# A six-stage decoder in one launch: denominators first in the cross-attention, keys waited for by group, POOL's turn 1 and F1's second pair reordered

## The reference, cut to what matters

```python
x = x + _L0_attn_ref(_layernorm(x), ...)     # A0: 16 heads, softmax(q k^T) v
x = x + _L0_xattn_ref(_layernorm(x), ...)    # X0: 16 heads of 8, 77 context rows, rotary positions
x = x + _L0_ffn_ref(_layernorm(x), ...)      # F0: router to 16 experts, top 2, capacity; 2 shared experts
x = x + _L1_attn_ref(_layernorm(x), ...)     # A1: 16 heads of 8, plus clipped relative positions
x = x + _L1_xattn_ref(_layernorm(x), ...)    # X1: one head over the context
x = x + _L1_ffn_ref(_layernorm(x), ...)      # F1: 8 dense experts weighted by a top-2 gate
```

```python
attn = jax.nn.softmax(scores, axis=-1)
out = jnp.einsum('bhqk,bhkd->bhqd', attn, v)
```

```python
attn = jnp.einsum('bhld,bhrd->bhlr', q, k) * scale
rel = jnp.einsum('bhld,lrd->bhlr', q, pos_emb) * scale
attn = jax.nn.softmax(attn + rel, axis=-1)
```

## Time and profile before

| | |
|---|---|
| runs | 1357.92, 1363.59, 1365.1 us (median 1363.59) |
| profiled execution | 1360.92 us, span 1358.6 us |
| mean granted PE clock | 0.962 |
| busy: PE, DVE, ACT, POOL | 1240.3, 984.2, 711.7, 650.1 us |
| chain that ended last | PE 65%, DVE 17%, ACT 6%, issue 4%, POOL 4% |
| instructions | 29396 |

### The profile page before, as it was taken

The page is one execution under the profiler, slowest core; times in us unless marked ns, Lnnn a source line. Parts: engine busy times, 40 slices in busy tenths (PEclk is TensorE's granted clock), DMA queues, the critical chain, the costliest instruction groups (busy, mean ns, idle before and its releaser), DMA issues.

```text
span 1358.6 us, 29396 instructions
## 1 busy us (share of the span) xinstructions
PE 1240.3 (91%) x10886; PEld 913.6 (67%) x10886; DVE 984.2 (72%) x2403; ACT 711.7 (52%) x1473; POOL 650.1 (48%) x786
## 2 busy tenths in 40 slices
PE   7999999999999989861849998999999999899998
PEld 5667667766776756540339766777777777677887
DVE  5888897788779778768425466687877879776554
ACT  4666656766666645620113345666656666533221
POOL 3555556555655631130456468876654755401110
PEclk9999999999999999975879999999999999999999
DMA  5241000000000020000014132321220211000001
GB/s 179 59 125 32 1 1 2 1 1 2 1 1 1 1 71 2 1 1 0 5 49 115 45 63 85 87 59 25 44 51 20 57 36 31 1 1 1 0 0 31
DMA packets 77048, 43.88 MB, mean 32 GB/s; under 512 B 26138, under 2 KB 71787, under 8 KB 76919
## 3 DMA queue, kind: packets, MB, share of 16 engines
q1 hardware_dynamic: 72438, 38.59, 11.0%
q10 hardware_dynamic: 2432, 2.28, 0.6%
q0 software_dynamic: 2048, 1.27, 0.4%
HBM read 21.91 MB, written 10.49 MB: 24 GB/s over the span
## 4 chain that ended last, share of the span: by engine, by line
PE 65%; DVE 17%; ACT 6%; issue 4%; POOL 4%; DMA 1%; SPq 1%; ACTq 0%; DVEq 0%; POOLq 0%
PE psum L1737 8%; PE psum L1314 7%; PE psum L1299 6%; PE psum L1846 6%; PE psum L1289 6%; PE psum L1749 4%; PE psum L1857 4%; PE psum L1721 4%; PE psum L1728 3%; ACT arena L937 2%; PE psum L1265 2%; POOL xs_rows L703 2%; PE psum L1564 2%; DVE arena L2258 2%; DVE negmax L2533 1%
## 5 line engine op out<-in xcount | busy, mean ns | idle before, releaser
L645 POOL TENSOR_TENSOR arena<-arena,rden 128x512 f32<-128x512 f32 x256 | 260.6, 1042 | 214.9 <-DVE rden L1992 214.8
L937 ACT ACTIVATE arena<-psum,negmax 128x512 f32<-128x512 f32 x256 | 175.1, 694 | 150.9 <-DVE negmax L1983 124.0
L2533 DVE TENSOR_REDUCE negmax<-psum 128x1 f32<-128x512 f32 x256 | 164.6, 685 | 49.3 <-PE psum L1728 44.2
L1983 DVE TENSOR_REDUCE negmax<-psum 128x1 f32<-128x512 f32 x256 | 168.1, 681 | 40.2 <-PE psum L1289 39.1
L1299 PEld LDWEIGHTS psum<-cst,arena 128*128 128x128 f32 x1024 | 112.6, 140 | 47.2 <-issue 46.5
L1299 PE MATMUL psum<-cst,arena 128*128 128x128 f32 x1024 | 139.3, 277 | 4.4 <-DVE arena L1978 0.8
L1289 PE MATMUL psum<-a_qk 64*128 64x512 f32 x768 | 106.0, 408 | 2.5 <-DVE a_qk L2001 2.5
L1846 PE MATMUL psum<-f_h,f_w 128*128 128x512 f32 x384 | 100.8, 411 | 5.1 <-DVE arena L2631 5.1
L1721 PE MATMUL psum<-a_kstack,a_qblk 96*128 96x512 f32 x256 | 96.0, 457 | 5.1 <-DMA a_kstack<-a_klo 3.9
L1195 ACT ACTIVATE arena<-psum 128x512 f32<-128x512 f32 x64 | 38.1, 597 | 106.2 <-PE psum L1846 106.1
L1289 PEld LDWEIGHTS psum<-a_qk 64*128 64x128 f32 x768 | 67.2, 184 | 39.1 <-issue 24.2
(11 more groups left out here) (361 smaller groups left out, 2845.2 us busy)
## 6 DMA issues: line engine op xcount, KB each, us to landing
w<-in_ew SPq DMA_DIRECT2D x2, 2048.0 KB, 8.7
a_kstack<-a_khi SPq DMA_DIRECT2D x64, 64.0 KB, 2.0
xs_rows<-f SPq DMA_DIRECT2D x3, 1024.0 KB, 5.3
ys_rows<-wqkv SPq DMA_DIRECT2D x8, 384.0 KB, 3.0
arena<-xs_rows SPq DMA_DIRECT2D x7, 384.0 KB, 3.8
a_kstack<-a_klo SPq DMA_DIRECT2D x32, 64.0 KB, 1.9
a_kstack<-a_khi SPq DMA_DIRECT2D x64, 32.0 KB
a_qstack<-a_qhi SPq DMA_DIRECT2D x121, 16.0 KB, 2.2
```

Of the source, the lines that this page charges most:

```text
L645: pool.tensor_tensor(a0_p[u % 4], a0_p[u % 4], rden[:, u:u + 1].broadcast_to([P, SEQ]), ALU.mult).then_inc(a0_norm, 1)
L937: act.activation(a0_p[u % 4], bank[u % 4][:, :], ACT.Exp, bias=negmax[:, u:u + 1], accum_out=den[:, u:u + 1]).then_inc(a0_exp, 1)
L1983: dve.tensor_reduce(negmax[:, u:u + 1], bank[u % 4][:, :], AX.X, ALU.max, negate=True).then_inc(a0_max, 1)
L2533: dve.tensor_reduce(negmax[:, n % 8:n % 8 + 1], bank[n % 4][:, :], AX.X, ALU.max, negate=True).then_inc(a1_max, 1)
```

## The change

It has four parts. **A:** in X0 from pair 1 on, the denominators are computed in the odd iteration, into bank 7, and the numerators in the even one; the output projection goes to the upper half of bank 6. The reciprocal waits for denominators alone, the multiply for both. In the router's order, turn(3) goes behind router(2). Two fills of two matmuls without use (`keep_busy`) are added on PE: one before the last tile's turns, one behind turn(2). **B:** in A1 the waits for keys are by group in all turns. **C:** POOL adds expert rows in turn 1 after values and low keys instead of before, and the statistics and their end on DVE are one step later there. **D:** DVE's pair 1 of F1 is written out, its first steps ahead of the last two additions of pair 0.

```diff
+        def x0_sums(u):
+
+            return bank[7][:, 0:UQ] if u else bank[6][:, UQ:2 * UQ]
...
         def keys_of_group(it, g):
 
-            own = ((a1_kfirst, 48), (setup, 6 + 48)), ((a1_kfirst, 96), (setup, 6 + 96), (a1_emb, 3 + 96))
-            return own[it][g] if it < 2 and g < len(own[it]) else keys_stacked(it)
+            if g == 0:
+                return a1_kfirst, 48 * it + 48
+            if g == 1:
+                return setup, 6 + 48 * it + 48
+            if g == 2 and it:
+                return a1_emb, 3 + 48 * it + 48
+            return a1_kin[it % 2], 48 * (it // 2) + (48 if it % 2 else 96)
...
-        SCALE_AT = {(it, 5): ("pre", b) for it, b in PRE_NORM.items()}
+        SCALE_AT = {(it, 6 if it == 1 else 5): ("pre", b) for it, b in PRE_NORM.items()}
...
                 if it:
-                    pool.wait_ge(*keys_stacked(it - 1))
-                if it and it < 3:
-                    for g in range(4 if it == 2 else 2):
+                    for g in range(HQ):
                         pool.wait_ge(*keys_of_group(it - 1, g))
...
                 stage_q(it, 1)
                 gather_one(it, 1)
-                if it == 1:
-                    add_experts(1)
                 stage_v(it)
                 gather_one(it, 2)
                 if it < NT - 1:
                     low_k(it + 1)
+                if it == 1:
+                    add_experts(1)
...
                 if t >= 4 and c == 0 and t % 2 == 0:
-                    act.wait_ge(x0_den, t // 2 - 1)
+                    act.wait_ge(x0_den, 2 * (t // 2 - 1))
...
+                    for g in range(HQ):
                         act.wait_ge(*keys_of_group(it - 1, g))
...
@@ -1418,19 +1419,25 @@
                 b = u // 2
                 if u == 0:
                     pe.wait_ge(x0_qr, 3)
-                pe.wait_ge(x0_tc, u * 8 + 8)
-                if u:
-                    pe.wait_ge(x0_norm, u)
+                    pe.wait_ge(x0_tc, 8)
+                else:
+                    pe.wait_ge(x0_x, 2 * u)
...
+                mm.then_inc(x0_den, 1)
 
             def x0_denominators(u):
+                if u:
+                    pe.wait_ge(x0_tc, u * 8 + 8)
+                    pe.wait_ge(x0_norm, u)
+                if u == 1:
+                    pe.wait_ge(x0_qr, 5)
...
-                        mm = pe.matmul(bank[6][32 * j:32 * j + 32, UQ:2 * UQ], x0_one[:, (3 - i) * HD:(7 - i) * HD],
+                        mm = pe.matmul(x0_sums(u)[32 * j:32 * j + 32, :], x0_one[:, (3 - i) * HD:(7 - i) * HD],
                                        x0_pT[u % 2][:, 4 * j + i, :], start=(i == 0), stop=(i == HQ - 1))
                 mm.then_inc(x0_den, 1)
...
@@ -1438,10 +1445,8 @@
                 pe.wait_ge(x0_norm, u + 1)
                 if u:
                     pe.wait_ge(x0_x, 2 * u)
-                else:
-                    pe.wait_ge(x0_qr, 5)
                 for t in range(2):
-                    o = bank[7][:, t * D:(t + 1) * D]
+                    o = bank[6][:, UQ + t * D:UQ + (t + 1) * D]
...
+                if t == NT:
+                    pe.wait_ge(x0_sub, NT)
+                    keep_busy(bank[3], 2)
...
                     if u == NT // 2:
                         f0_router(1)
                         f0_turn(2)
+                        keep_busy(bank[5], 2)
+                        f0_router(2)
                         f0_turn(B - 1)
-                        f0_router(2)
                         f0_router(B - 1)
                     if 0 <= u < NT // 2:
-                        x0_numerators(u)
+                        (x0_denominators if u else x0_numerators)(u)
                 elif 0 <= u < NT // 2:
-                    x0_denominators(u)
+                    (x0_numerators if u else x0_denominators)(u)
...
-                if p == 0 or it < 2 and p % 2 == 0:
+                if p % 2 == 0:
                     pe.wait_ge(*keys_of_group(it, p // 2))
...
             def x0_normalise(u):
-                dve.wait_ge(x0_den, u + 1)
-                ln(dve.reciprocal(x0_rden, bank[6][:, UQ:2 * UQ]))
+                dve.wait_ge(x0_den, 2 * u + 1 if u else 2)
+                ln(dve.reciprocal(x0_rden, x0_sums(u)))
                 if u:
                     dve.wait_ge(x0_o, u)
+                dve.wait_ge(x0_den, 2 * u + 2)
                 dve.tensor_tensor(x0_f, bank[6][:, 0:UQ], x0_rden, ALU.mult).then_inc(x0_norm, 1)
...
-                dve.tensor_tensor(xu, xu, bank[7][:, 0:UQ].rearrange("p (t d) -> p t d", t=2), ALU.add).then_inc(x0_x, 2)
+                dve.tensor_tensor(xu, xu, bank[6][:, UQ:2 * UQ].rearrange("p (t d) -> p t d", t=2), ALU.add).then_inc(x0_x, 2)
...
+                late = it == 1
+                if it in PRE_NORM and p - late in (4, 5):
+                    pre_stats(PRE_NORM[it], 2 * (p - late) - 8, 2 * (p - late) - 6)
...
             dve.wait_ge(g_chain, 500)
+            f1_hid(1, 0)
+            f1_hid(1, 1)
             add(0, 6)
+            f1_hid(1, 2)
             add(0, 7)
-            with dve.Fori(1, E1 // 2) as i:
+            f1_hid(1, 3)
+            add(1, 0)
+            for k in range(2, 8):
+                f1_hid(1, 2 * k)
+                f1_hid(1, 2 * k + 1)
+                add(1, k - 1)
+            add(1, 7)
+            with dve.Fori(2, E1 // 2) as i:
                 for k in range(8):
                     f1_hid(i, 2 * k)
                     f1_hid(i, 2 * k + 1)
```

More of the change, by code:

```diff
@@ L390, in decoder_kernel @@
         UH = UN // 2
+        def x0_sums(u):
+            return bank[7][:, 0:UQ] if u else bank[6][:, UQ:2 * UQ]
         def stacked(per_turn, it):
             return per_turn[it % 2], (it // 2 + 1) * STACK - (it + 1) % 2 * 96
-        def keys_stacked(it):
-            return a1_kin[it % 2], (it // 2 + 1) * STACK - (144 if it % 2 else 96)
         def keys_of_group(it, g):
-            own = ((a1_kfirst, 48), (setup, 6 + 48)), ((a1_kfirst, 96), (setup, 6 + 96), (a1_emb, 3 + 96))
-            return own[it][g] if it < 2 and g < len(own[it]) else keys_stacked(it)
+            if g == 0:
[5 more added lines that the diff above has]
+            return a1_kin[it % 2], 48 * (it // 2) + (48 if it % 2 else 96)
         def key_parts(it):
@@ L1119, in high_k @@
                     act.wait_ge(a1_klo, it)
-                    act.wait_ge(*keys_stacked(it - 1))
-                if it and it < 3:
-                    for g in range(4 if it == 2 else 2):
+                    for g in range(HQ):
                         act.wait_ge(*keys_of_group(it - 1, g))
@@ L2377, in pre_stats_of @@
             def pre_stats_of(it, p):
-                if it in PRE_NORM and p in (4, 5):
-                    pre_stats(PRE_NORM[it], 2 * p - 8, 2 * p - 6)
+                late = it == 1
+                if it in PRE_NORM and p - late in (4, 5):
+                    pre_stats(PRE_NORM[it], 2 * (p - late) - 8, 2 * (p - late) - 6)
             def pre_part(b, part):
```

## The result

The kernel after takes 1354.28 us (median of 6 runs, 1350.84 to 1355.71), the one before 1362.23 (6 runs): a ratio of 0.9942, 95% interval 0.9925 to 0.9960, or 7.9 us less. Forecast were 1355.5 and a gain of 6.8. A second set of runs gave 1353.71 and 0.9939 (0.9917 to 0.9961).

What follows compares the result with a forecast made beforehand. PE, busy 91% of the span, bounds the kernel, besides serial chains where it idles. Terms -2.2 - 0.3 - 0.85 - 3.4 = -6.8 gave 1354.1 from the profiled run, 1356.8 from the median; 1355.5 was taken, range 1349.5 to 1362.

Steps and rivals of the forecast that it cites:

- A, -2.2: X0 and router: earlier denominators and new router order start the bisection 2.2 us earlier; bounds -1.1 and -3.7.
- The cap by POOL: Router: POOL's reduction moves by 1.6 only and ends 0.67 before L2240, so the bisection moves at most 2.3.
- The first fill: End of X0: two matmuls take 1.76 us, so the last turns begin 0.4 earlier where 1.4 was possible.
- C and B in turn 2, -0.3: A1 turn 2: waits of 1.67 and 3.03 become one 4 us stop on POOL's ln_h; net -0.3, bounds -1.4 and +0.3.
- the wait for vtok: A1 turn 2: PE's wait of 1.67 before L1737 goes, since DVE's statistics move one step later.
- The step that failed: A1 turn 2: if the clock falls again behind the 4 us stop, 1.1 us is paid behind L1642 instead.
- B in turn 4, -0.85: A1 turn 4: PE's wait of 0.88 for the whole key stack goes by group; -0.85, bounds 0 and -0.88.
- The many added waits: A1's later turns: three more already met waits on PE each, taken to cost 0, at the other end +2.1.
- D, -3.4: F1 pair 1: PE's gap of 2.55 becomes 0.7 (-1.8), and 1.6 of lost clock returns; bounds -1.8 and -3.4.
- The stops only move: Rival in X0, A1, F1: A -1.1, turn 2 0, B -0.85, D -1.8; together -3.8, about 1358.5; chance 0.32.
- POOL is not the limit: Rival in router and A1: A -3.7, turn 2 -5.8, with B and D -13.7, about 1349; chance 0.08.
- The slower side: Rival in A1: group waits add clock falls of 1.6 to 1.7 us; over eight give 1369; chance 0.04.

Runs made afterwards that it cites:

- e7: Kernel after with POOL's split of the first two experts' weights behind the reduction over partitions instead of ahead of it; ratio 0.9933 (0.9913 to 0.9952).
- e1: Kernel before with part A alone (denominators first, both fills, router's new order); ratio 0.9971 (0.9958 to 0.9983).
- e4: Kernel after without its two fills on PE; ratio 0.9921 (0.9899 to 0.9943).
- second profile: Kernel after itself, unchanged, profiled again on the same chip in the same rounds as two later experiments; no separate ratio given for it.
- e2: Kernel before with parts B and C alone (keys by group, POOL's low keys ahead of additions, statistics a step later); ratio 0.9984 (0.9974 to 0.9995).
- e8: Kernel before with part B alone (waits for keys by group), POOL's order untouched; ratio 0.9993 (0.9975 to 1.0011).
- e3: Kernel before with part D alone (F1's pair 1 written out, its products ahead of the last additions); ratio 0.9984 (0.9969 to 0.9999).
- e9: Kernel after with next sequence's projections one place later in turns 2 and 3, no first fill, POOL's split behind the scatter; ratio 0.9900 (0.9875 to 0.9924).
- e11: e9 with one small POOL multiply of 128x8 elements directly behind the reduction; 1345.73 us, ratio 0.9876 (0.9856 to 0.9896).

## Why the prediction was right, point by point

The time, the sign and the size were right; the terms were less even than their sum, and part of the agreement is luck. Forecast were -2.2 (A), -0.3 (turn 2), -0.85 (turn 4) and -3.4 (D). In the profile of the kernel after they are -2.6, +1.0, -1.3 and -3.9, with +0.4 between the bisection and A1.

- **A, -2.2.** The profiles show -2.6 and -2.5 up to the bisection. The places were right to 0.4 us: turns at 575.79 (forecast 575.9), output(6) at 579.55 (579.8), output(7) at 586.30 (586.6). The cap by POOL held as a mechanism. Its size was too small: "the reduction on POOL ... moves by 1.6 only" became 2.0 (from 607.15 to 605.16), and with the slack of 0.67 that is the 2.67 measured. What the prediction did not see is the larger cost of POOL's chain: its splits slow DVE's rows, although rows of 1.05 and 1.30 us stand among those of 0.42 in the profile before. e7 showed that the router's start had 2.7 more to give. The time of e1, -3.9 with an interval of -5.7 to -2.3, holds the 2.5 of its profile; whether more than that is real is not settled.
- **The first fill.** It was forecast to hold the last turns to 0.4 where 1.4 were to be had. Measured 1.0 in e4: right.
- **C and B in turn 2, -0.3.** The waits came out much as described: one of 4.56 on POOL's ln_h (forecast 4.0), behind it half clock, no wait for keys. That the wait for vtok "goes" was too much, 0.53 is left. POOL's way to ln_h became 1.6 shorter instead of 1.1, because the values and low keys filled the 1.56 in which POOL had waited for a gathered row, and no wait was left behind them; in the second profile a wait of 1.32 for PE stands there instead and only 0.4 is won. The step that failed is the clock. The sum had the half clock behind the stop and no further fall, and bounds of -1.4 and +0.3; measured up to turn 3 is +1.0 in the kernel after, +2.8 in its second profile and +1.3 in e2, all with the fall near 856 to 862 as well. Without that fall (e4, e7) it is -0.2 and +0.4. All of e2 measured -2.2 (-3.5 to -0.7) against -1.15 forecast for B and C, which its one profile, with nothing won, doesn't show.
- **B in turn 4, -0.85.** Turn 4 lost its wait; the way from turn 3's first scores to turn 4's became 1.3 shorter, and 1.1 in e8. The many added waits cost nothing that shows: the rest of A1 takes 273.04 against 273.10 (one fall of the clock less, one longer, about 1.7 each).
- **D, -3.4.** The profile shows -3.9, e3's -3.6. Of this 1.8 is the gap, as forecast, and the rest was the clock (2.1, forecast 1.6), which the prediction took as always lost before. It is not: in e1 and e8, with the same gap, F1 takes 164.9, two less than in before. The four profiles without D average 165.8 and the ten with it 163.3, so the mean of the term is nearer -2.5, and e3 measured -2.2 (-4.2 to -0.1).
- **The rivals.** "The stops only move" was right for turn 2 and wrong for X0 and F1. "POOL is not the limit" fell: PE waited for ln_h in every run with keys by group that left PE's turn at its place. The slower side, more clock falls by the new rhythm, came at most once, near 856; the falls in the rest of A1 vary between executions.

## What to carry to other kernels

When two waits in a row are taken away, look up what the next instruction waits for before counting them: here POOL's LayerNorm took most of both, and moving its consumer by one step was worth more (6.4 us of a profile) than the whole reordering of POOL's work ahead of it. DVE rows two or three times as long as their neighbours of the same form pointed here to POOL's work at that moment; moving that work helped only to a place where neither engine was needed. The first fill of the matrix engine covered 0.7 us of waiting and cost the other 1.0 of its length, so try a kernel without its fills.

## What the runs showed of the hardware

- DVE's TENSOR_TENSOR of 128x256 takes 0.42 us alone and 0.92 to 1.34 beside POOL's TENSOR_TENSOR (before, after); a SCALAR_TENSOR_TENSOR of 128x3 takes 0.22 alone and 0.96 to 1.10 (e7). A TENSOR_REDUCE of 0.42 beside it (598.59 in the kernel after) and the TENSOR_SCALAR_CACHE_REDUCE rows of 0.47 in e7 keep their length.
- POOL's reduction over partitions costs twice: 5.5 to 5.7 us without work before it, and 7.5 to 7.6 before the first ordinary arithmetic behind it (e7, e9, e11). Scatter DMAs and a memset in between run without paying the second (e9). What POOL does in either stretch no row shows. The Trainium skill, "GPSIMD Engine Reference", section on instruction dispatch, gives about 6 us for a first call into freshly loaded code; the way there agrees, the way back is longer here.
- The same idle gap of PE of 2.53 to 2.56 us in the same place of the program was followed by half clock in two profiles of four. After a stop of 4.56 it was at half clock before PE started again, and with the stop filled it stayed at full.
